# Splitting a weight load in three and moving the clearing transfers in an attention kernel

## The chip, the cores and the metric

The kernel runs on one core of one Trainium2 chip. The metric is the time of one launch in microseconds (us). The core has five instruction streams that run side by side and meet at semaphores: TensorE (PE, matrix products and transposes), VectorE (DVE), ScalarE (ACT), GpSimd (POOL) and SyncE (SP), which computes nothing here and issues most of the DMAs. "SPq" in a row is SP's stream; each stream is worked off strictly in its order.

## The reference

One decoder layer on x of 8 x 112 tokens x 512, in float32:

```python
x = _layernorm(x + attn(x, ...))     # latent attention: 16 heads, query rank 384, latent 128, rope part 64
x = _layernorm(x + xattn(x, ctx))    # cross-attention, 16 heads
x = _layernorm(x + ffn(x))           # 16 routed experts, the best 2 per token, and 2 shared experts

# inside attn
q_c, kv_c = rms_norm(x @ wq_down.T), rms_norm(x @ wkv_down.T)
q = concat(q_c @ wq_up.T, rope(q_c @ wq_rope.T)); k, v from kv_c @ wkv_up.T and rope(x @ wk_rope.T)
out = softmax(mask(q k^T * scale)) v @ wo.T
```

## The kernel before

Every float32 operand of a product is split into a high part (a rounding copy, nearly always on ACT) and a low part (source minus high part, nearly always on DVE), and a product is three matmuls: high x high, high x low, low x high. A weight thus goes HBM, buffer `stage`, high part, low part, product.

The first attention works on four groups of four heads (`NG = 4`, `GH = 4`). The weights of a group come in two loads into the one buffer `stage`: `wa`, 2816 columns of 128 partitions (1408 KB: the rope part of the query, the query's up-projection, the key's up-projection), and after it `wb`, 2560 columns (1280 KB: values and output). They are split in three pieces each:

```python
A_PIECES = [(0, A_UP), (A_UP, A_UP + 1024), (A_UP + 1024, A_SIZE)]   # 0:768, 768:1792, 1792:2816
B_PIECES = [(B_V, B_O), (B_O, B_O + 2 * D), (B_O + 2 * D, B_SIZE)]   # 0:512, 512:1536, 1536:2560
```

The order of the work of each engine is written out by hand, in lists of items (`ATT_PE`, `ATT_ACT`, `ATT_DVE`, `ATT_POOL`, lines 138 to 166). The list runs three times as the body of a loop, and a last list (`ATT_LAST_...`) ends the stage. In a body an item that is marked NEXT belongs to the next group: its weights are fetched and split while the present group's heads are still worked on. The items that matter here:

- `SA` 0 to 2: the split of the three pieces of `wa`; the high part on ACT counts `a_hi`, the low part on DVE counts `a_lo`. In ACT's body the next group's `SA` 0 and `SA` 1 stand next to each other, ahead of the transpose copy `T` 2.
- `SB` 0 to 2: the split of the three pieces of `wb`; the low part counts `bw_lo`. `SB` 0 of a group stands near the end of a body, `SB` 1 and `SB` 2 near the start of the next.
- `O` 0 and `E` 0 of the next group: the products that make the rope part of the queries, odd and even. They read piece 0 of `wa` (`a_lo` of one piece), and are PE's first work that needs the new weights. In PE's order `G` 3, `G` 4, `Z` 1, `S` 3, `S` 4, `T` 2 and `G` 5 come right ahead of `O` 0, then `B` 3, `Z` 2, `S` 5, `E` 0.
- `R` 0 and `R` 1: the split of one half (448 tokens) of the rotated queries into `ro_hi` (ACT) and `ro_lo` (POOL, which counts `rot_lo`). Each waits until the half before has been carried away (`pack_ld`).
- `G` j: scores of batch j. `G` 0 to 3 need the packed rope half 0 of their group, `G` 4 to 7 half 1.

SP's stream for this stage stands in lines 534 to 575. Ahead of the loop it issues the inputs, then `wa` of group 0 in one DMA (line 544), the residual input `acc` (line 545), `wb` of group 0, and `pack(0, 0)` and `pack(0, 1)`. `pack(g, half)` waits for `rot_lo` and issues 16 small DMAs (56 KB each, line 555) which carry a rotated half into `qr`. Then for g = 1, 2, 3:

1. wait until all three pieces of the old `wb` are split (line 569), then `wa` of group g in one DMA (line 570);
2. `load_b(g)`: wait until all three pieces of `wa` are split, then `wb` in one DMA (line 561);
3. `pack(g, 0)` and `pack(g, 1)`;
4. ten DMAs of 256 KB (`NZERO = 10`, line 575), HBM to HBM, that clear rows of `rows_in`, which the routed experts use much later (POOL waits for `zero_st` at line 781).

After the loop SP loads the weights of the cross-attention into `stage` (lines 589 to 591) and its context. `st_ld` is one semaphore for all `wa` and `wb` loads, counted up by 16 each.

Of the kernel before, what the change touches and what calls it, by code (L numbers as in the profile page):

```python
# [40 lines left out]
NZERO = -(-NBLK // (NG - 1))  # L41
# [275 lines left out]
def build(nc, d, rows_in, rows_out, out):  # L317
    with ExitStack() as ctx:
# [6 lines left out]
        def sem(name):  # L325
            return ctx.enter_context(nc.semaphore(name))
# [62 lines left out]
        def gap(name, upto):  # L389
# [70 lines left out]
        ix_i = sb("ix_i", [P, NBLK], I32)  # L460


        xo_ld, x2_ld, wk_ld, c_ld, acc_ld, st_ld, cx_ld, b_ld, zero_st, sc_st, out_st = map(
            sem, "xo_ld x2_ld wk_ld c_ld acc_ld st_ld cx_ld b_ld zero_st sc_st out_st".split())
        x_ld = [sem(f"x_ld{k}") for k in range(KD)]
        w_ld = [sem(f"w_ld{k}") for k in range(KD)]
        one_set, fw0_hi, fw0_lo = map(sem, "one_set fw0_hi fw0_lo".split())
        kb_ld = [sem(f"kb_ld{half}") for half in range(2)]
        pack_ld = [sem(f"pack_ld{half}") for half in range(2)]
        f_ld = [sem(f"f_ld{i}") for i in range(2)]  # L470
# [63 lines left out]
        @block.sync  # L534
        def _(sp):
            for k in range(KD):
                sp.dma_start(wd[:, k, 0:D], d["wdown"][:, k, 0:D]).then_inc(w_ld[k], 16)
                sp.dma_start(xT[:, k, 0:HALF], d["xT"][:, k, 0:HALF]).then_inc(x_ld[k], 16)
            sp.dma_start(xT[:, :, HALF:T], d["xT"][:, :, HALF:T]).then_inc(x2_ld, 16)
            sp.dma_start(wd[:, :, D:768], d["wdown"][:, :, D:768]).then_inc(wk_ld, 16)  # L540
            for dst, name in ((ident, "ident"), (maskf, "mask"), (wnorm, "wnorm")):
                sp.dma_start(dst[:, :], d[name]).then_inc(c_ld, 16)
            sp.dma_start(tab[:, :, :], d["tab"]).then_inc(c_ld, 16)
            sp.dma_start(stage[:, 0:A_SIZE], d["wa"][0, :, :]).then_inc(st_ld, 16)
            sp.dma_start(acc[:, :, :], d["xN"]).then_inc(acc_ld, 16)

            def pack(g, half):


                sp.wait_ge(rot_lo, 2 * g + half + 2)  # L550
                for part, src in enumerate((ro_hi, ro_lo)):
                    for o in range(2):
                        for h in range(GH):
                            row = 64 * part + 32 * o
                            sp.dma_start(  # L555
                                f32(qr[row:row + 32, h, half * HALF:(half + 1) * HALF]),
                                f32(src[32 * h:32 * h + 32, o, :])).then_inc(pack_ld[half], 16)

            def load_b(g):
                sp.wait_ge(a_lo, g * len(A_PIECES) + len(A_PIECES))  # L560
                sp.dma_start(stage[:, 0:B_SIZE], d["wb"][g, :, :]).then_inc(st_ld, 16)

            load_b(0)
            sp.wait_ge(kr_done, 4)
            pack(0, 0)
            pack(0, 1)
            with sp.Fori(1, NG) as g:

                sp.wait_ge(bw_lo, g * len(B_PIECES))
                sp.dma_start(stage[:, 0:A_SIZE], d["wa"][g, :, :]).then_inc(st_ld, 16)  # L570
                load_b(g)
                pack(g, 0)
                pack(g, 1)
                for i in range(NZERO):
                    sp.dma_start(rows_in[i, g - 1, :, :], d["zeros"]).then_inc(zero_st, 16)  # L575

            def load_x(g, lo, hi, loaded):
                sp.dma_start(stage[:, lo:hi], d["wx"][g, :, lo:hi]).then_inc(loaded, 16)

            def spread_keys(g, half):  # L580

                sp.wait_ge(x_free["K"], XJ.count(("K", half), g))
                for h in range(GH):
                    r = slice(DXH * h, DXH * (h + 1))
                    sp.dma_start(f32(kb[r, half, :, :, h, :]).rearrange("p a b s -> p (a b) s"),
                                 f32(kx[r, half, :, :]).rearrange("p a (b s) -> p (a b) s", b=HB))\
                      .then_inc(kb_ld[half], 16)

            sp.wait_ge(bw_lo, NG * len(B_PIECES))
            load_x(0, 0, X_O, xl_ld)  # L590
            load_x(0, X_O, X_SIZE, xo_ld)

            sp.wait_ge(a_free["B"], NG * GH)
            sp.dma_start(cx[:, :, :], d["ctxT"][:, :, 0:S]).then_inc(cx_ld, 16)
            sp.wait_ge(kz_set, 1)
            sp.wait_ge(a_free["G"], NG * B)
            for half in range(2):
                for a in range(2):
                    sp.dma_start(f32(kb[:, half, a, :, :, :]).rearrange("p b h s -> p b (h s)"),
                                 f32(kz[:, :]).unsqueeze(1).broadcast_to([P, HB, GH * S])).then_inc(kb_zero[half], 16)  # L600
            sp.wait_ge(kb_zero[0], 32)
            spread_keys(0, 0)

            sp.wait_ge(a_free["W"], 1 + NG * TT)
            for s in range(2):
                sp.dma_start(w1f[:, s, :], d["wf"][s, :, :]).then_inc(f_ld[s], 16)
            sp.wait_ge(kb_zero[1], 32)
            spread_keys(0, 1)
            with sp.Fori(1, NG) as g:
                sp.wait_ge(xl_lo, g)  # L610
                load_x(g, 0, X_O, xl_ld)
                spread_keys(g, 0)
                sp.wait_ge(xo_lo, g)
                load_x(g, X_O, X_SIZE, xo_ld)
                spread_keys(g, 1)

            sp.wait_ge(xl_lo, NG)
            sp.wait_ge(xo_lo, NG)
            for dst, name in ((gw[:, :, :], "gw"), (gb[:, :], "gb"),
                              (rev[:, :], "rev"), (e2[:, :], "e2"), (rt_c[:, :], "route")):  # L620
                sp.dma_start(dst, d[name]).then_inc(b_ld, 16)
            with sp.Fori(1, 2 * NF) as i:
                for s in range(2):

                    sp.wait_ge(fw_lo, 2 * i + s + 1)
                    sp.dma_start(stage[:, s * ROW:(s + 1) * ROW], d["wf"][2 * i + s, :, :])\
                      .then_inc(f_ld[s], 16)
            for t in range(TT):
                sp.wait_ge(ln_out, 2 * len(ROWS_ON_DVE) + t + 1)
                sp.dma_start(out[:, t, :], acc2[:, t, :]).then_inc(out_st, 16)  # L630
            sp.wait_ge(out_st, 16 * TT)
# [181 lines left out]
        def _(act):  # L813
# [36 lines left out]

            squares(0)
            act.wait_ge(in_lo, 2 * KD + 2)
            act.wait_ge(st_ld, 16)
            for lo, hi in A_PIECES:
                copy(wa_hi[:, lo:hi], stage[:, lo:hi]).then_inc(a_hi, 1)
            for b in range(HB):
                values(b)
# [38 lines left out]
            def att_step(item, g, at):  # L896
# [23 lines left out]
                    copy(ro_hi[:, :, :], rt[:, :, :]).then_inc(rot_hi, 1)  # L920
                elif kind == "SA":
                    lo, hi = A_PIECES[j]
                    act.wait_ge(st_ld, 32 * g + 16)
                    copy(wa_hi[:, lo:hi], stage[:, lo:hi]).then_inc(a_hi, 1)
                elif kind == "SB":
                    if j == 0:
                        act.wait_ge(st_ld, 32 * g + 32)

                        act.wait_ge(a_free["A"], AJ.count(("A", KQ - 1), g))
                    elif j == 1:  # L930

                        act.wait_ge(job_done, AJ.base(g))
                    copy(part_b(j, wa_hi, ws_hi), stage[:, slice(*B_PIECES[j])]).then_inc(bw_hi, 1)
                elif kind == "S":
                    probabilities(B * g + j, j)
                elif kind == "T":
                    transposed(B * g + j, j)
                elif kind == "Z":
                    act.wait_ge(z_done, B * g + j + 1)
                    copy(ZT_hi[:, :, j * S:(j + 1) * S],  # L940
                         ps[:, 4 + j % 2, 0:GH * S].rearrange("p (h s) -> p h s", h=GH))\
                        .then_inc(z_hi, 1)

                elif kind == "CX":
                    act.wait_ge(a_free["B"], NG * GH)
                    act.wait_ge(cx_ld, 16)
                    copy(cx_hi[:, :, :], cx[:, :, :]).then_inc(cxs_hi, 1)
                elif kind == "L":
                    split_l(0)
                elif kind == "ROOT1":  # L950
                    layernorm_root(0, j)
                elif kind == "ROW1":
                    row(0, j)
                elif kind == "SQRT":
                    function_ready(ACT.Sqrt)
                elif kind == "U1":
                    turned(0, j, x1T_hi)
                elif kind == "K":
                    x_step(item, 0, at)
# [1053 lines left out]
```

## Time and profile before

| | us |
|---|---|
| median of three runs | 851.8 |
| lowest and highest | 851.23, 852.64 |
| the profiled execution | 852.53 |
| its span | 850.7 |
| PE busy in the span | 820.5 |
| DVE, ACT, POOL busy | 531.7, 456.6, 241.2 |

The span is from the first to the last instruction of the profiled execution; its time has 1.83 us more. Busy PE is counted with modelled ends of pipelined matmuls: a matmul with 448 columns is listed with 0.36 us, but the next starts 0.20 us after it. Start-to-start times are therefore the ones to read on PE. "DMA to landing" is from the issue of a DMA until its semaphore says it is done. The granted clock is given as a share of 2.4 GHz.

### The profile page before, as it was taken

The page shows a single profiled execution, that of the slowest core. Times are in us where ns is not written, and L with a number is a line of the kernel's source. Part 1 is how long each engine was busy: PE and PEld are TensorE (multiplying, and loading weights), DVE is VectorE, ACT ScalarE, POOL GpSimd, SP SyncE. Part 2 cuts the span into 40 slices and gives each one's busy share as a digit, 9 for nine tenths or more (in the row PEclk, how much of TensorE's full clock was granted, in tenths as well). Part 3 has the DMA queues.
Part 4 walks back from the last instruction along what each step waited for, and adds up shares of the span by engine and source line. Part 5 has one row for each costly group of instructions (what it writes and reads, how often), then busy time and mean ns, then how long its engine had stood idle before and what let it go on. Part 6 is the DMA issues. An engine that isn't in the chain of part 4 may idle for free.

```text
span 850.7 us, 13303 instructions
## 1 busy us (share of the span) xinstructions
PE 820.5 (96%) x4270; PEld 700.7 (82%) x4270; DVE 531.7 (63%) x994; ACT 456.6 (54%) x1189; POOL 241.2 (28%) x284
## 2 busy tenths in 40 slices
PE   7999999799899999999997999999999999999997
PEld 5887888688688888888885888888888888889885
DVE  4757756654564677687787657265655655646466
ACT  6427535443554466977786616153755737547050
POOL 0142311032132132655654003502232322321420
PEclk9999999899989999999999999999999999999999
DMA  9113214230611346333112204534554655644422
GB/s 340 67 44 112 68 40 129 106 105 21 213 62 43 86 135 201 92 68 74 37 21 69 75 25 133 214 109 139 190 195 134 233 168 171 201 147 137 134 76 87
DMA packets 41598, 99.99 MB, mean 118 GB/s; under 512 B 15889, under 2 KB 23953, under 8 KB 39921
## 3 DMA queue, kind: packets, MB, share of 16 engines
q1 hardware_dynamic: 30496, 61.62, 22.9%
q0 software_dynamic: 11056, 37.79, 13.6%
q8 instruction: 27, 0.44, 0.2%
q14 instruction: 19, 0.15, 0.1%
HBM read 71.59 MB, written 20.97 MB: 109 GB/s over the span
## 4 chain that ended last, share of the span: by engine, by line
PE 78%; SPq 7%; DVE 4%; DMA 4%; ACT 3%; issue 3%; POOL 1%; DVEq 0%; ACTq 0%; POOLq 0%
PE ps L1549 63%; SPq L555 4%; DMA stage<-in_wa 3%; PE ps L1896 2%; PE ps L1570 2%; PE ps L1609 2%; PE ps L1712 2%; PE ps L1886 1%; SPq L575 1%; PE ps L1780 1%; ACT Pt L886 1%; POOL ro_lo L700 1%; DMA kb<-kx 1%; PE ps L1898 1%; PE ps L1720 1%
## 5 line engine op out<-in xcount | busy, mean ns | idle before, releaser
L641 POOL TENSOR_TENSOR Pt<-Pt,rowinv 112x448 f32<-112x448 f32 x64 | 59.6, 935 | 183.4 <-DVE rowinv L1153 183.2
L886 ACT ACTIVATE Pt<-ps,negmax 112x112 f32<-112x112 f32 x256 | 87.2, 358 | 26.9 <-DVE negmax L1146 26.4
L1549 PE MATMUL ps<-x2T_hi,ws_hi 128*128 128x448 f32 x256 | 95.2, 372 | 1.7 <-DVE x2T_lo L1090 1.7
L1549 PE MATMUL ps<-x2T_hi,ws_lo 128*128 128x448 f32 x256 | 93.6, 366 | 0.0
L1549 PE MATMUL ps<-x2T_lo,ws_hi 128*128 128x448 f32 x256 | 93.6, 366 | 0.0
L1549 PE MATMUL ps<-w_hi,h_hi 128*128 128x512 f32 x224 | 89.9, 401 | 0.0
L1549 PE MATMUL ps<-w_hi,h_lo 128*128 128x512 f32 x224 | 88.4, 395 | 0.0
L1549 PE MATMUL ps<-w_lo,h_hi 128*128 128x512 f32 x224 | 88.4, 395 | 0.0
L1017 ACT ACTIVATE hf<-ps,b 128x448 f32<-128x448 f32 x64 | 40.6, 634 | 88.0 <-PE ps L1549 68.7
L1090 DVE TENSOR_TENSOR h_lo<-hf,h_hi 128x448 fp32r<-128x448 f32 x64 | 39.9, 624 | 45.5 <-ACT h_hi L1018 45.0
L1435 DVE TENSOR_TENSOR acc<-ps,acc 128x512 f32<-128x512 f32 x56 | 38.5, 689 | 45.4 <-PE ps L1549 37.7
L1549 PE MATMUL ps<-qkT_hi,wa_hi 128*128 128x448 f32 x144 | 55.9, 388 | 11.0 <-DVE wa_lo L1090 9.5
L765 POOL DMA_INDIRECT wg<-in_wtab,ix_i x29 | 31.0, 1070 | 112.1 <-DVE ix_i L1420 61.3
L1163 DVE TENSOR_TENSOR acc<-ps,acc 128x512 f32<-128x512 f32 x56 | 38.6, 690 | 25.8 <-PE ps L1549 25.7
L815 ACT ACTIVATE PT_hi<-ps 112x448 fp32r<-112x448 f32 x64 | 34.7, 544 | 36.1 <-PE ps L1609 35.9
L1549 PE MATMUL ps<-qkT_hi,wa_lo 128*128 128x448 f32 x144 | 53.9, 374 | 0.0
L1549 PE MATMUL ps<-qkT_lo,wa_hi 128*128 128x448 f32 x144 | 53.8, 374 | 0.0
L886 ACT ACTIVATION_READ_ACCUMULATOR Pt<-ps,negmax 112x1 f32 x256 | 53.7, 210 | 0.0
L1549 PEld LDWEIGHTS ps<-x2T_hi,ws_hi 128*128 128x128 f32 x256 | 48.1, 188 | 6.5 <-POOL ws_lo L649 2.1
L1549 PEld LDWEIGHTS ps<-x2T_lo,ws_hi 128*128 128x128 f32 x256 | 48.2, 188 | 4.4
L1549 PEld LDWEIGHTS ps<-x2T_hi,ws_lo 128*128 128x128 f32 x256 | 48.1, 188 | 4.0
L1549 PEld LDWEIGHTS ps<-w_hi,h_lo 128*128 128x128 f32 x224 | 42.1, 188 | 10.2
(289 smaller groups left out, 2215.0 us busy)
## 6 DMA issues: line engine op xcount, KB each, us to landing
stage<-in_wf SPq DMA_DIRECT2D x30, 513.0 KB
rows_in<-in_zeros SPq DMA_DIRECT2D x30, 256.0 KB, 3.8
xs<-rows_in POOLq DMA_DIRECT2D x29, 256.0 KB, 4.2
rows_out<-yb POOLq DMA_DIRECT2D x29, 256.0 KB
stage<-in_wa SPq DMA_DIRECT2D x4, 1408.0 KB, 8.1
stage<-in_wb SPq DMA_DIRECT2D x4, 1280.0 KB, 5.5
qr<-ro_hi SPq DMA_DIRECT2D x64, 56.0 KB, 1.9
qr<-ro_lo SPq DMA_DIRECT2D x64, 56.0 KB, 1.9
```

The costliest lines, as they stand in the source:

```text
L555: sp.dma_start(f32(qr[row:row + 32, h, half * HALF:(half + 1) * HALF]), f32(src[32 * h:32 * h + 32, o, :])).then_inc(pack_ld[half], 16)
L641: nc.gpsimd.tensor_tensor(p, p, rowinv[0:S, b % 2, :].unsqueeze(2).broadcast_to([S, GH, S]), ALU.mult).then_inc(norm_done, 1)
L765: return pool.indirect_dma_start(dst, None, table, bass.IndirectOffsetOnAxis(ap=index, axis=0))
L815: return nc.scalar.activation(dst, src, ACT.Copy, **kw)
L886: last = nc.scalar.activation(Pt[0:S, b % 2, h * S:(h + 1) * S], ps[0:S, b % 2, h * S:(h + 1) * S], ACT.Exp, bias=negmax[0:S, b % 2, h:h + 1],
L1017: nc.scalar.activation(hf[:, q % 4, :], ps[:, q % 3, 0:HALF], ACT.Gelu, bias=bias)
L1090: return nc.vector.tensor_tensor(dst, src, f32(hi), ALU.subtract)
L1163: nc.vector.tensor_tensor(acc[:, t, :], ps[:, 6 + at.bank, :], acc[:, t, :], ALU.add)\
L1435: V.tensor_tensor(acc2[:, t, :], ps[:, 3 + m % 2, :], (acc2 if n else acc)[:, t, :], ALU.add)\
L1549: ins = mm(dst, w, x, start=start and i == 0, stop=stop and i == len(ops) - 1, skip_group_check=not (start and stop))
L1570: ins = mm(ps[0:S, b, :], w, x, start=k == 0 and i == 0, stop=k == KD - 1 and i == 2, skip_group_check=True)
L1609: ins = nc.tensor.transpose(ps[0:S, 2 + b % 2, h * S:(h + 1) * S], Pt[0:S, b % 2, h * S:(h + 1) * S], ident[0:S, 0:S])
```

## The change

The one DMA for `wa` of a group becomes three, one for each of `A_PIECES`, each with a semaphore of its own (`sa_ld[j]`). Inside the loop each of them waits only until those pieces of the old `wb` that lie under it are split: two for piece 0, all three for pieces 1 and 2. ACT waits per piece instead of for the whole. `wb` gets the semaphore `sb_ld`. The ten clearing DMAs move from the end of the loop's body to between `load_b(g)` and `pack(g, 0)`.

```diff
-            sp.dma_start(stage[:, 0:A_SIZE], d["wa"][0, :, :]).then_inc(st_ld, 16)
+            for (lo, hi), arrived in zip(A_PIECES, sa_ld):
+                sp.dma_start(stage[:, lo:hi], d["wa"][0, :, lo:hi]).then_inc(arrived, 16)
...
-                sp.dma_start(stage[:, 0:B_SIZE], d["wb"][g, :, :]).then_inc(st_ld, 16)
+                sp.dma_start(stage[:, 0:B_SIZE], d["wb"][g, :, :]).then_inc(sb_ld, 16)
...
-                sp.wait_ge(bw_lo, g * len(B_PIECES))
-                sp.dma_start(stage[:, 0:A_SIZE], d["wa"][g, :, :]).then_inc(st_ld, 16)
+                for j, (lo, hi) in enumerate(A_PIECES):
+                    under = sum(b < hi for b, _ in B_PIECES)
+                    sp.wait_ge(bw_lo, (g - 1) * len(B_PIECES) + under)
+                    sp.dma_start(stage[:, lo:hi], d["wa"][g, :, lo:hi]).then_inc(sa_ld[j], 16)
                 load_b(g)
+                for i in range(NZERO):
+                    sp.dma_start(rows_in[i, g - 1, :, :], d["zeros"]).then_inc(zero_st, 16)
                 pack(g, 0)
                 pack(g, 1)
-                for i in range(NZERO):
-                    sp.dma_start(rows_in[i, g - 1, :, :], d["zeros"]).then_inc(zero_st, 16)
...
-            act.wait_ge(st_ld, 16)
-            for lo, hi in A_PIECES:
+            for j, (lo, hi) in enumerate(A_PIECES):
+                act.wait_ge(sa_ld[j], 16)
                 copy(wa_hi[:, lo:hi], stage[:, lo:hi]).then_inc(a_hi, 1)
...
-                    act.wait_ge(st_ld, 32 * g + 16)
+                    act.wait_ge(sa_ld[j], 16 * g + 16)
...
-                        act.wait_ge(st_ld, 32 * g + 32)
+                        act.wait_ge(sb_ld, 16 * g + 16)
```

## Rows read from the trace of the kernel before

**Rows 1.** The page, part 1: busy time of each engine.

```profile
PE 820.5 (96%) x4270; PEld 700.7 (82%) x4270; DVE 531.7 (63%) x994; ACT 456.6 (54%) x1189; POOL 241.2 (28%) x284
```

**Rows 2.** Chain of waits, 45 to 330 us: start, duration, what.

```profile
128.09 0.95 ACT ro_hi L815
...
149.24 7.82 DMA stage<-in_wa
```

**Rows 3.** Timeline of SP: start, duration, engine, line, operation, count.

```profile
8.80 0.57 SPq L544 DMA_DIRECT2D stage<-in_wa  x1
...
77.18 0.36 SPq L570 DMA_DIRECT2D stage<-in_wa  x1
95.12 0.34 SPq L561 DMA_DIRECT2D stage<-in_wb  x1
104.16 4.95 SPq L555 DMA_DIRECT2D qr<-ro_hi  x8
...
131.43 4.94 SPq L555 DMA_DIRECT2D qr<-ro_hi  x8
...
141.64 6.94 SPq L575 DMA_DIRECT2D rows_in<-in_zeros  x10
...
206.79 4.94 SPq L555 DMA_DIRECT2D qr<-ro_hi  x8
...
282.24 4.95 SPq L555 DMA_DIRECT2D qr<-ro_hi  x8
```

**Rows 4.** Timeline of PE: first matmuls of `G` 4, `G` 5 and `O` 0.

```profile
83.98 0.44 PE L1712 MATMUL ps<-qa_hi,qkT_hi 128*112 128x448 f32 x1
...
85.25 0.47 PE L1549 MATMUL ps<-qkT_hi,wa_hi 128*128 128x448 f32 x1
...
150.22 0.37 PE L1712 MATMUL ps<-qa_hi,qkT_hi 128*112 128x448 f32 x1
...
153.19 0.44 PE L1712 MATMUL ps<-qa_hi,qkT_hi 128*112 128x448 f32 x1
...
158.97 0.74 PE L1549 MATMUL ps<-qkT_hi,wa_hi 128*128 128x448 f32 x1 [4.54 <-DVE wa_lo L1090]
...
228.52 0.44 PE L1712 MATMUL ps<-qa_hi,qkT_hi 128*112 128x448 f32 x1
...
234.75 0.74 PE L1549 MATMUL ps<-qkT_hi,wa_hi 128*128 128x448 f32 x1 [4.99 <-DVE wa_lo L1090]
```

**Rows 5.** Windows: PE, PEld, DVE, ACT, POOL busy; granted clock; DMA share; GB/s.

```profile
143.00:155.00 12.00, 11.41 (x65) 9.11 (x63) 8.92 (x16) 6.84 (x24) 1.87 (x2) 1.00 0.95 328
155.00:160.00 5.00, 1.03 (x3) 0.94 (x4) 2.02 (x3) 2.92 (x8) 0.00 (x0) 0.66 0.06 25
```

**Rows 6.** Timelines of DVE and of ACT: splits of `stage`.

```profile
139.70 1.22 DVE L1090 TENSOR_TENSOR ws_lo<-stage,ws_hi 128x1024 fp32r<-128x1024 f32 x1
143.44 1.22 DVE L1090 TENSOR_TENSOR ws_lo<-stage,ws_hi 128x1024 fp32r<-128x1024 f32 x1
...
19.68 2.73 ACT L815 ACTIVATE wa_hi<-stage 128x768 fp32r<-128x768 f32 x3
...
83.36 1.80 ACT L815 ACTIVATE wa_hi<-stage 128x768 fp32r<-128x768 f32 x2 [1.28 <-DMA stage<-in_wa]
...
157.09 1.79 ACT L815 ACTIVATE wa_hi<-stage 128x768 fp32r<-128x768 f32 x2 [5.79 <-DMA stage<-in_wa]
```

**Rows 7.** DMA issues by line: KB of each, median us to landing.

```profile
stage<-in_wx SPq DMA_DIRECT2D x4, 384.0 KB, 3.7
...
stage<-in_wa SPq DMA_DIRECT2D x1, 1408.0 KB, 9.5
...
rows_in<-in_zeros SPq DMA_DIRECT2D x10, 256.0 KB, 3.9
...
stage<-in_wb SPq DMA_DIRECT2D x1, 1280.0 KB, 5.6
```

More of the change, by code:

```diff
@@ L460, in build @@
         ix_i = sb("ix_i", [P, NBLK], I32)
-        xo_ld, x2_ld, wk_ld, c_ld, acc_ld, st_ld, cx_ld, b_ld, zero_st, sc_st, out_st = map(
-            sem, "xo_ld x2_ld wk_ld c_ld acc_ld st_ld cx_ld b_ld zero_st sc_st out_st".split())
+        xo_ld, x2_ld, wk_ld, c_ld, acc_ld, sb_ld, cx_ld, b_ld, zero_st, sc_st, out_st = map(
+            sem, "xo_ld x2_ld wk_ld c_ld acc_ld sb_ld cx_ld b_ld zero_st sc_st out_st".split())
         x_ld = [sem(f"x_ld{k}") for k in range(KD)]
@@ L467, in build @@
         one_set, fw0_hi, fw0_lo = map(sem, "one_set fw0_hi fw0_lo".split())
+        sa_ld = [sem(f"sa_ld{j}") for j in range(len(A_PIECES))]
         kb_ld = [sem(f"kb_ld{half}") for half in range(2)]
```

## The prediction

> **What bounds the kernel now.** I read the page first. PE is busy 820.5 of 850.7 us [rows 1], so only stretches in which PE stands still or runs slowly can give anything. Next the chain of waits, cut to the first attention: nearly all of it is PE, but in the second and the third body it leaves PE, goes along SP's small pack DMAs, then along the ten clearing DMAs, then into the load of `wa` [rows 2]. The timeline of SP says why: the clearing DMAs are issued from 141.64 to 148.58, and only then `wa`, at 149.24 [rows 2, 3]. It lands 7.82 us later, at 157.06. ACT has waited for it 5.79 us, and PE 4.54 us in this body and 4.99 us in the third [rows 4, 6]. In the first body nothing clears ahead of `wa` (issue at 77.18), ACT waits 1.28 us, and PE shows no idle time worth a mark [rows 3, 4, 6].
>
> PE pays once more after the wait: the granted clock of 155 to 160 us is 0.66, a mix of 1.2 and 2.4 GHz, where it was 1.00 before [rows 5]; PE had stood still for 4.54 us.
>
> The whole loss of a body can be read without separating the two. From the first matmul of `G` 5 to the first pack DMA of the next half, SP's start at 131.43, the three bodies do the same work: 131.43 - 83.98 = 47.45 us, 206.79 - 153.19 = 53.60, and 282.24 - 228.52 = 53.72 [rows 3, 4]. Against the first body the second loses 6.15 us and the third 6.27. The other part of the period is even: `G` 5 to `G` 5 is 69.21 us from the first body to the second and 75.33 from the second to the third, and these differ by 6.12, the same loss.
>
> **The change, part by part.** *Clearing DMAs out of the way of `wa`.* Once they are gone, SP is past its last pack DMA at about 141.5 (the next instruction begins at 141.64 [rows 3]). Piece 0 needs `SB` 0 and `SB` 1 of the old group split: the low part of `SB` 1 ends at 139.70 + 1.22 = 140.92 [rows 6], so piece 0 goes at about 141.7. Pieces 1 and 2 need `SB` 2, which ends at 143.44 + 1.22 = 144.66 [rows 6], so they go at 144.8 and, one issue of 0.36 [rows 3] and a wait later, at 145.3. Nothing else is queued on SP behind these waits but `load_b`, which in the first body came 95.12 - 77.18 = 18 us after the load of `wa` [rows 3].
>
> *When the pieces land.* Piece 0 has 384 KB; DMAs of that size took 3.7 us [rows 7], so it is there at 145.4. Pieces 1 and 2 are 1024 KB together, less than the 1280 KB of `wb`, which took 5.6 us [rows 7]: they are there by 150.4 at the latest for piece 1 and by 150.9 for piece 2. ACT comes to `SA` 0 at 157.09 - 5.79 = 151.30 and to `SA` 1 some 0.85 us later [rows 6]. So ACT waits for none. The slack is 5.9 us for piece 0 and 1.7 us for piece 1; piece 2 is split some 10 us later. Bounds of this step: nothing is left to wait for, or, if piece 1 landed as slowly as the whole `wa` does behind the clearing (7.82 us from 144.8), it is there at 152.6 and ACT loses 0.5 us per body, which also is late for nothing on PE but `E` 0. I take no wait.
>
> *What is late next.* Ahead of `O` 0 PE has `G` 5 (five matmuls, 0.20 us start to start and the first a little slower, about 1.1 us), and can start `O` 0 at about 154.3. ACT's high part of piece 0 would end at about 152.2; DVE's low part follows in its order behind other splits. In the first body the same order left 85.25 - 83.98 = 1.27 us between the two starts [rows 4], against 1.10 for the matmuls alone: 0.17 us lost with ACT 1.28 us late. The second and third bodies therefore come to the pace of the first, and slightly below it. Gain: 6.15 + 6.27 = 12.42 us, the slower clock included, since PE no longer stands still before these products.
>
> *The first body, and what the yardstick itself loses.* Here `wa` is issued at 77.18 behind the pack DMAs, not the clearing. Piece 0 lands at about 80.9 instead of 83.3, piece 1 at about 82 to 83; ACT comes to `SA` 0 at 82.08 [rows 3, 6, 7]. ACT's 1.28 us of waiting goes, all but some tenths. On PE that is worth at least the 0.17 us seen at `O` 0 and at most 1.28. The same amount is to be added in the other two bodies, for they were measured against this one. Three times 0.17 to 1.28 is 0.5 to 3.8 us; I take 0.4 each, nearer to the row at PE, 1.2 us in all.
>
> *Clearing DMAs in their new place.* `wb` is issued at 95.12, and SP then waited for `rot_lo` until 104.16 [rows 3]. Ten clearing DMAs take 6.94 us of issue [rows 3], from about 95.7 to 102.8. They fit with 1.3 us to spare, three times, as the distance between the two issues is set by PE's order. If that cover were gone, SP would be late with `pack(g, 0)`, which has 10.2 us of issue (131.43 to 141.64 is a whole pack [rows 3]), so ends near 114.5 to 115.5 and lands some 2 us later. The first who needs it is `R` 1 on ACT at 128.09 [rows 2], so about 11 us of cover stand behind the 1.3. Also the transfers: 1280 KB of `wb` and 2560 KB of clearing are 3.93 MB; at the 328 GB/s of a stretch full of such transfers [rows 5] that is 12.0 us, done at about 108. The pack DMAs issued from 104.16 stand behind them for up to 4 us, and the last ones, issued at 114 to 115, no longer. Cost 0.
>
> The rule that speaks against this change is in the Trainium skill, page "SBUF — State Buffer", section "The DMA setup-cost knee": each transfer pays some 2 us whatever its size, so one should coalesce. If the price were paid in series, an estimate from its fit (2 us + size / 436 GB/s) has pieces 1 and 2 at 144.8 + 2 x 3.2 = 151.2, still ahead of ACT's 152.15 for piece 1, and the sum stands. The trace disagrees with a series here: the clearing DMAs are issued every 0.70 us and land after 3.9 us each.
>
> *The start.* `wa` of group 0 becomes three DMAs: SP issues two more, at 0.57 us each [rows 3], so `acc` is asked for 1.1 us later; it is added to first in the loop, tens of us later. The whole `wa` landed at 8.80 + 9.5 = 18.3 [rows 3, 7], ACT took it from 19.68, and its third piece near 21.3 [rows 6]. Landing up to 1.1 us later is covered. Cost 0; without the cover it would be 1.1 us at most. A gain is excluded: ACT was busy with other work until 19.68.
>
> *The end of the stage.* In the last pass the clearing also stood in front of the cross-attention's weights (issue near 300.7). They come earlier now, but no engine was seen waiting for them. Worth 0. Semaphore renames cost nothing, and two more waits per group on ACT stand ahead of copies whose data is there.
>
> **Sum.** 12.42 + 1.2 = 13.6 us off the profiled execution: span 850.7 - 13.6 = 837.1, plus the 1.83 us around it 838.9. That execution lies 0.7 above the median of the runs shown (852.53 against 851.8), so the forecast for a median is 838.2. Nothing behind the stage depends on absolute time: it begins 13.6 us earlier and PE is the bound there as well.
>
> **Rivals.** *A, a part of the wait survives.* Piece 1 or DVE's low part comes late, or another wait inside ACT's order appears once PE no longer pauses (the pause let DVE and ACT catch up). For it: with ACT 1.28 us late `O` 0 was already late by 0.17 us, so the order has little over 1 us of slack there [rows 4, 6]. Against it: the first body shows the pace with ACT 1.3 us late. Half a us to 2 us per body at the place of the old wait, without the slow clock: 12.42 + 1.2 - 3 x 1.2 = 10.0 off, 841.8.
>
> *B, slower than before: the pack DMAs starve behind the clearing.* In the new place the clearing stands ahead of `pack(g, 0)` in the same queue. If HBM to HBM transfers were served one after another at their 3.9 us [rows 7], they would end at 100.7 + 39 = 140, the pack at about 142, and `R` 1 on ACT, due at 128.09 [rows 2], would be 14 us late; `pack(g, 1)` then is issued from about 145 and lands at 157, where `G` 4 wants it at 150.22 [rows 4]: PE loses about 7 us there beside what ACT's delay costs it before, say 12 in each of three groups, +36 - 13.6 = +22, 874. It decides from the point at which the backlog passes 11 us (the cover of `R` 1), and turns the sign when PE loses 4.5 us per group. Against it: the clearing DMAs are issued every 0.70 us and the `wa` behind all ten landed after 7.82 us, about 2 more than the 5.6 of a load of like size alone [rows 2, 7]: the backlog was 2 us, not 30. By the page's fit in series each would cost an estimated 2.6 us and the clearing 26, so the same would happen in a milder form.
>
> *C, the change does not remove the wait*, because `bw_lo` and not the clearing holds `wa`. Against it: `SB` 2 was split at 144.66, and `wa` issued at 149.24 [rows 3, 6]. If all pieces waited for it and landed only after the full 7.82 us, ACT would be served at 152.6, 1.3 us late, as in the first body: 12.4 us off, 839.4. So C lies inside the forecast's own bounds, and is no case of its own. That nothing is gained at all (within 0.2%) needs a second cost that eats 12 us, and I see none.
>
> **How the numbers follow.** Forecast 0.80, A 0.16, B 0.02, nothing gained 0.02. The forecast's own bounds are nothing and 3.8 beside the 12.42, so 839.4 to 835.6, and about 0.7 for the spread of medians. Range 836 to 841: it takes the forecast and the better half of A. A change of 0.2% (1.7 us) is what a measurement can tell from none. Faster 0.96, same 0.02, slower 0.02.
>
> **What would show it.** In the profile after: the three `wa` DMAs directly behind the pack DMAs, the second one about 3 us after the first in bodies two and three; the ten clearing DMAs behind `wb`; no wait of ACT for `stage<-in_wa` and none of PE for `wa_lo` above 0.3 us; `G` 5 to the next pack at 47 us in all three bodies; granted clock 1.00 there. It would be wrong if PE showed a new wait, above all for `pack_ld` at `G` 4 or for `wa_lo` at `E` 0, if ACT waited at `R` 1, or if the later stages took longer than the 850.7 - 282.2 = 568.5 us that they take from the third body's pack on.

## The result, and the profile after

The changed kernel took 838.58 us (median of four runs, 837.5 to 839.28), the kernel before 851.98 beside it (851.23 to 852.64): ratio 0.9837, 95% interval 0.9822 to 0.9851. In two further groups of runs the same kernel had 839.42 and 838.59 us, against 853.07 and 853.74 of the kernel before (ratios 0.984, interval 0.9822 to 0.9858, and 0.9818, interval 0.9804 to 0.9832). The forecast was 838.2 us, range 836 to 841.

The profiled execution took 837.5 us with a span of 835.7 us, 15.0 less than before. PE's busy time hardly changed, its share did (page, part 1, of the kernel after; compare [rows 1]):

```profile
PE 816.4 (98%) x4270; PEld 698.3 (84%) x4270; DVE 530.9 (64%) x994; ACT 456.7 (55%) x1189; POOL 241.1 (29%) x284
```

The timeline of SP of the kernel after, as in [rows 3]:

```profile
76.73 1.49 SPq L574 DMA_DIRECT2D stage<-in_wa  x3
93.78 0.33 SPq L563 DMA_DIRECT2D stage<-in_wb  x1
94.33 7.38 SPq L577 DMA_DIRECT2D rows_in<-in_zeros  x10
102.81 4.98 SPq L557 DMA_DIRECT2D qr<-ro_hi  x8
...
130.08 4.94 SPq L557 DMA_DIRECT2D qr<-ro_hi  x8
135.06 5.02 SPq L557 DMA_DIRECT2D qr<-ro_lo  x8
140.77 3.56 SPq L574 DMA_DIRECT2D stage<-in_wa  x3
...
198.65 4.94 SPq L557 DMA_DIRECT2D qr<-ro_hi  x8
...
267.17 4.95 SPq L557 DMA_DIRECT2D qr<-ro_hi  x8
```

Three things are to be seen. The load of `wa` stands right behind the pack DMAs, at 140.77 where it was at 149.24. The three pieces take 3.56 us to issue in body two, since the second waits for `SB` 2. And the issue of the clearing DMAs ends at 101.71, 1.1 us before the pack that follows them.

The timeline of PE of the kernel after: `G` 5 of the three bodies and `O` 0 of the first, as in [rows 4].

```profile
83.25 0.44 PE L1716 MATMUL ps<-qa_hi,qkT_hi 128*112 128x448 f32 x1
...
84.34 0.37 PE L1553 MATMUL ps<-qkT_hi,wa_hi 128*128 128x448 f32 x1
...
151.81 0.44 PE L1716 MATMUL ps<-qa_hi,qkT_hi 128*112 128x448 f32 x1
...
220.36 0.44 PE L1716 MATMUL ps<-qa_hi,qkT_hi 128*112 128x448 f32 x1
```

From `G` 5 to the first pack DMA of the next half it is now 130.08 - 83.25 = 46.83, 198.65 - 151.81 = 46.84 and 267.17 - 220.36 = 46.81 us, against 47.45, 53.60 and 53.72 before [rows 3, 4]. That is 0.62 + 6.76 + 6.91 = 14.3 us. Behind the third body's pack the span has 835.7 - 267.17 = 568.53 us more, before it was 568.46: in this profile the gain is kept to the end (other profiles lose 1.1 us of it there, see e3 below). The remaining 0.7 of the 15.0 us come from an earlier start (first `wb` load at 25.76 instead of 26.50), which is looked at below.

In body two ACT takes both pieces from `stage` without waiting (timeline of ACT of the kernel after, as in [rows 6]), and the clock holds (a window, columns as in [rows 5]). The other two bodies show no wait for `stage` either.

```profile
149.79 1.81 ACT L819 ACTIVATE wa_hi<-stage 128x768 fp32r<-128x768 f32 x2
```

```profile
155.00:160.00 5.00, 5.00 (x29) 4.20 (x28) 4.65 (x9) 2.26 (x4) 0.36 (x1) 1.00 0.00 0
```

### The profile page after: what moved, and what is told of

It reads as the page before. It is cut to its first block, busy times and chain, and to the rows that moved or that the text cites. A ratio compares the mean times of both kernels' runs of the same rounds, so it can differ in the third digit from the quotient of the medians.

```text
span 835.7 us, 13323 instructions
## 1 busy us (share of the span) xinstructions
PE 816.4 (98%) x4270; PEld 698.3 (84%) x4270; DVE 530.9 (64%) x994; ACT 456.7 (55%) x1189; POOL 241.1 (29%) x284
## 4 chain that ended last, share of the span: by engine, by line
PE 89%; DVE 4%; ACT 3%; issue 1%; DMA 1%; SPq 1%; DVEq 0%; ACTq 0%
PE ps L1553 71%; PE ps L1716 4%; PE ps L1900 2%; PE ps L1574 2%; PE ps L1613 2%; PE ps L1890 2%; PE ps L1724 1%; PE ps L1784 1%; ACT Pt L890 1%; DMA kb<-kx 1%; PE ps L1902 1%; SPq L589 1%; DVE stats L1173 1%; PE ps L1568 1%; PE ps L1605 0%
## 5 line engine op out<-in xcount | busy, mean ns | idle before, releaser
L1553 PE MATMUL ps<-qkT_hi,wa_hi 128*128 128x448 f32 x144 | 54.2, 377 | 1.3 <-DVE wa_lo L1097 0.6
```

Of the source, the lines that this page charges most:

```text
L1553: ins = mm(dst, w, x, start=start and i == 0, stop=stop and i == len(ops) - 1, skip_group_check=not (start and stop))
```

## Experiments

All are timed against the kernel before on the same chip, and each trace shown is one execution. Theory A is the prediction's: what cost the time was how late `wa` arrived against ACT, because of the clearing ahead of it on SP.

### One half of the change at a time

**after_again** is the changed kernel once more.

> The changed kernel once more, on the same chip as the three that follow, as their yardstick. Both theories: 838.6 us again, within 1 us. Beyond that: its first `wb` load was issued at 25.76 us where the kernel before had 26.50. If that 0.74 us belongs to the change, it is there again; if it is scatter between executions, the issue may come anywhere between 25.7 and 26.6.

839.42 us (839.31 to 840.06), ratio 0.984 (0.9822 to 0.9858).

**e1_clear_only**: the kernel before, with only this edit.

```diff
                 load_b(g)
+                for i in range(NZERO):
+                    sp.dma_start(rows_in[i, g - 1, :, :], d["zeros"]).then_inc(zero_st, 16)
                 pack(g, 0)
                 pack(g, 1)
-                for i in range(NZERO):
-                    sp.dma_start(rows_in[i, g - 1, :, :], d["zeros"]).then_inc(zero_st, 16)
```

> Only the clearing DMAs are moved, `wa` stays one DMA behind all of the old `wb`. Theory A (the clearing ahead of `wa` in SP's queue was the whole cause): `wa` goes about 4.6 us earlier against PE's order, when `SB` 2 is split, and lands 6.2 us later, within 0.5 us of when ACT comes for it. Bodies two and three run at the pace of the first, and the first keeps ACT's 1.3 us wait: some 0.65 us per body worse than the full change at most, so 838.8 to 840.6 us. Theory B (the early first piece carries the gain): PE still waits 3 us or more for `wa_lo` in bodies two and three, 845 us or more.

839.12 us (837.75 to 839.59), ratio 0.9832 (0.9813 to 0.9851): all of the gain that can be measured. SP's and ACT's timelines of this kernel:

```profile
65.38 4.95 SPq L555 DMA_DIRECT2D qr<-ro_hi  x8
...
130.68 4.95 SPq L555 DMA_DIRECT2D qr<-ro_hi  x8
144.09 0.34 SPq L570 DMA_DIRECT2D stage<-in_wa  x1
...
199.25 4.94 SPq L555 DMA_DIRECT2D qr<-ro_hi  x8
```

```profile
150.39 1.81 ACT L815 ACTIVATE wa_hi<-stage 128x768 fp32r<-128x768 f32 x2
```

The one load goes as soon as `SB` 2 is split, at 144.09, and it lands 6.0 us later; ACT begins at 150.39 with no idle time marked before it, so the cover is only 0.3 us.

These two traces also say what the clearing did to `wa`. Counted from the first pack DMA of the half before, `wa` is issued at 13.41 us here and at 17.81 us in the kernel before, 4.4 us later, because SP issues the clearing first; and it lands after 7.82 us there against 6.0 here, 1.8 us more, while the clearing's own bytes are moved. No run issued the clearing from another engine's stream, so these two parts are read from the traces and not separated by an experiment.

From pack to pack body two takes 199.25 - 130.68 = 68.57 us, exactly as in the full change (198.65 - 130.08 = 68.57). In the first body ACT still waits 1.3 us, and its pack to pack time is 65.30 us; the kernel before had 65.27, the full change 64.67. So the split into three is worth 0.6 us in the trace, once, which is less than the runs can tell. In bodies two and three e1 has all of the gain without the split (its third body takes 68.59 us, the full change 68.52).

**e2_split_only**: the changed kernel with the clearing DMAs back at the end of the body.

> Only the split into three DMAs, the clearing DMAs stay at the end of the loop's body. Theory A: all three pieces are issued behind the clearing, the first lands some 5 us later instead of 7.8, so ACT waits about 2.7 us and PE about 1.6 us in bodies two and three; the clock may still fall. Of the 14 us some 8 to 10 come back: 842 to 844.5 us. Theory B: the first piece is early enough whatever stands ahead of it, 839 us or less.

847.22 us (845.72 to 849.22), ratio 0.9931 (0.9911 to 0.995). This missed the expected 842 to 844.5, on theory A's side of the line but with less gain. ACT's, then PE's timeline of body two:

```profile
154.92 0.84 ACT L819 ACTIVATE wa_hi<-stage 128x768 fp32r<-128x768 f32 x1 [3.72 <-DMA stage<-in_wa]
```

```profile
156.81 0.47 PE L1553 MATMUL ps<-qkT_hi,wa_hi 128*128 128x448 f32 x1 [2.46 <-DVE wa_lo L1094]
```

The first piece was issued at 149.17 and ACT could begin 5.7 us later, where I had reckoned with 5; with nothing ahead of it such a piece lands 3.1 us after its issue (below). PE stands 2.46 us in body two and 2.20 in body three instead of the 1.6 reckoned, and the clock falls as well (0.76 in the five us from 155, 0.90 in the next five). From pack to pack the two bodies take 4.3 and 4.0 us more than in the changed kernel.

The Trainium skill, page "Perfetto Trace Analysis", section "DMA Optimizations", says that splitting a DMA can let the work complete sooner if the DMA engines are generally idle. The runs here do not bear out that condition: with the DMA engines 0.95 busy from 150 to 155 us the split won back 5.9 of 14 us, and with the clearing gone 0.6. With the clearing gone there was little left to win: ACT's 1.28 us of waiting in the first body.

**e3_first_whole**, and once more as **e3_again**: the changed kernel, with only the first load, ahead of the loop, in one DMA again (ACT's waits follow it, not shown).

```diff
-            for (lo, hi), arrived in zip(A_PIECES, sa_ld):
-                sp.dma_start(stage[:, lo:hi], d["wa"][0, :, lo:hi]).then_inc(arrived, 16)
+            sp.dma_start(stage[:, 0:A_SIZE], d["wa"][0, :, :]).then_inc(sa_ld[0], 16)
```

> The changed kernel, but `wa` of group 0 in one DMA as before; the loop is untouched. If the 0.74 us by which the start came earlier belongs to the split of the first load, this kernel is 0.7 us slower than the changed one and issues its first `wb` at about 26.5 us. If it was scatter, the two are the same within 0.3 us. Both theories on the clearing: no difference in the bodies, 68.5 us each.

837.83 us (837.27 to 838.97), ratio 0.9824 (0.9805 to 0.9843). Its first `wb` load was issued at 25.84 us, and in e1, which also has the whole first load, at 25.73; the changed kernel had 25.76 in one profile and 26.27 in the next. The earlier start does not belong to the split. The time, however, lay 1.6 us below that of the changed kernel beside it, which neither expectation had, so both were run again:

> The changed kernel as the yardstick of this group: 838 to 839.5 us. Its profile before had 1.2 us more between the last load ahead of the routed layer and the first output DMA (384.6 us against 383.3 in all others). If that belongs to single executions, it may be there or not; the kernel with the first load whole (next) is then equal to this one within 0.5 us.

> The changed kernel with `wa` of group 0 in one DMA, once more: in its first group of runs it had 837.83 us against 839.42 of the changed kernel. If the split of the first load costs something (descriptors while the DMA engines are full), it is again 1 us or more faster than the yardstick. If that was scatter of where a program's runs fall, the two lie within 0.5 us.

838.59 us (837.33 to 839.34) for the changed kernel, 838.74 (837.48 to 839.11) for the other: no difference, ratios 0.9818 (0.9804 to 0.9832) and 0.9822 (0.9809 to 0.9836). What remains is a scatter of about 1.1 us behind the third body: from its pack to the end it is 568.3 to 568.6 us in six profiles (the kernel before, the changed kernel's first, e1, e2 and both of e3) and 569.5 to 570.1 in the other six (the changed kernel's other two and e4 to e7).

The clock goes with it. In the two us from 176 us behind the pack, at the end of the cross-attention, the granted clock is 0.50 to 0.62 in the second six and 1.00 in the first six. Three of the first six have a slow stretch 4 us earlier, three have none. The window at 176 us in the changed kernel's first profile, then in its third (columns as in [rows 5]):

```profile
443.17:445.17 2.00, 1.80 (x9) 0.97 (x7) 1.97 (x5) 1.41 (x3) 1.84 (x4) 1.00 0.00 0
```

```profile
443.96:445.96 2.00, 2.00 (x9) 1.81 (x8) 1.37 (x3) 1.46 (x3) 1.84 (x4) 0.50 0.00 0
```

So the same kernel has its slow stretch at one place or 4 us later, and only the profiles with the later one have the longer end. That is read from twelve profiles side by side; no experiment moved the stretch, and what places it stays open.

### How much lateness costs what

**e4_half**: the kernel before, with five of the ten clearing DMAs moved behind `load_b` and five left.

> `wa` in one DMA, five of the ten clearing DMAs moved behind `load_b`, five left at the end of the body. Theory A (what counts is how late `wa` arrives against ACT): five DMAs are 3.5 us of issue, so `wa` goes at about 145 in body two and lands some 7 us later, at 152 to 152.5; ACT came for it at 149.8, so it waits 2.2 to 2.7 us, PE some 1.5 us, and the clock stays up or falls for part of a us. Loss against the changed kernel 1.5 to 2.5 us in each of two bodies and 0.6 in the first: 842 to 844 us. If a clearing DMA cost in proportion (theory C: 7.2 us per body for ten), it would be 845.5 us.

844.84 us (843.11 to 846.13), ratio 0.9889 (0.9873 to 0.9906), a little above theory A's range and by time alone as near to the proportional theory C. Within the kernel the two bodies differ. SP's timeline, then PE's in body two and body three:

```profile
131.61 4.96 SPq L555 DMA_DIRECT2D qr<-ro_hi  x8
141.83 3.39 SPq L577 DMA_DIRECT2D rows_in<-in_zeros  x5
145.89 0.34 SPq L570 DMA_DIRECT2D stage<-in_wa  x1
...
202.17 4.94 SPq L555 DMA_DIRECT2D qr<-ro_hi  x8
...
274.41 4.95 SPq L555 DMA_DIRECT2D qr<-ro_hi  x8
```

```profile
156.01 0.47 PE L1551 MATMUL ps<-qkT_hi,wa_hi 128*128 128x448 f32 x1 [1.39 <-DVE wa_lo L1092]
```

```profile
227.05 0.47 PE L1551 MATMUL ps<-qkT_hi,wa_hi 128*128 128x448 f32 x1 [1.87 <-DVE wa_lo L1092]
```

The windows of the two bodies, columns as in [rows 5]:

```profile
155.00:160.00 5.00, 3.90 (x20) 3.31 (x21) 4.05 (x8) 4.26 (x13) 0.93 (x1) 1.00 0.00 0
225.00:230.00 5.00, 3.13 (x11) 2.64 (x11) 2.83 (x5) 4.00 (x12) 0.93 (x1) 0.79 0.00 0
```

Against 68.5 us of the changed kernel, body two takes 202.17 - 131.61 = 70.56, 2.0 more, and body three 72.24, 3.7 more. `wa` landed 8.2 us after its issue in body two (7 had been reckoned) and 8.8 us in body three; ACT waited 2.64 and 3.12 us, and PE stood for 1.39 and 1.87. That is 0.5 us of the difference of 1.7. The larger part is the clock: 1.00 all through 155 to 165 us, but 0.79 and 0.87 in the two stretches of five us from 225. From the fourth matmul of `O` 0 on, the same ten matmuls up to the start of the tenth take 1.91 us in body two (156.73 to 158.64) and 3.43 in body three (227.76 to 231.19), 1.5 us more, of which 0.3 is won back at `E` 0, where body two waits and body three does not. Half the clearing in front thus costs 2.0 us in a body when the clock holds and 3.7 when it does not; all of it costs 6.8 and 6.9. The profiled execution was the slowest of the four, 846.13 us with a mean granted clock of 0.993; the fastest had 843.11 with 0.997. So theory A's range holds where the clock holds; what the expectation had too small is the cost of the clock.

**e5_wait_all**: the changed kernel, every piece waits for the whole of the old `wb`.

```diff
-                    under = sum(b < hi for b, _ in B_PIECES)
+                    under = len(B_PIECES)
```

> The changed kernel, but all three pieces of `wa` wait until the whole of the old `wb` is split, so that the first piece goes 3 us later, at 143.4 in body two, and lands near 146.5; ACT comes for it at 149.8. Theory A: no difference, 838.6 us within 0.7. If the early first piece matters, PE or ACT shows a wait and the time rises by 1 us or more.

838.57 us (837.66 to 839.43), ratio 0.9834 (0.9817 to 0.985): no difference. `wa` went at 144.15 instead of 140.77 and nobody waited for it. The finer wait of the first piece is worth nothing here.

### The cover behind the clearing

**e6_clear_x2** and **e7_clear_x4** have twenty and forty clearing DMAs per body in the new place; `rows_in` is made larger, and the new ones clear spare rows.

```diff
-                for i in range(NZERO):
+                for i in range(4 * NZERO):
```

> The changed kernel with twenty clearing DMAs in place of ten in each body, the ten new ones into spare rows that nothing reads. SP is busy with them for 14 us, so `pack(g, 0)` goes about 5.5 us later than in the changed kernel and lands at about 120 in body one; `R` 1 on ACT comes for it at 127. Theory A (11 us of cover behind the pack): no difference, 838.6 us within 0.7. Theory D (the clearing costs by its traffic or by starving the pack DMAs, the rival of the prediction): 3 us or more slower.

838.47 us (837.58 to 840.29), ratio 0.9827 (0.981 to 0.9844): twice the clearing is free. The pack moved from 102.81 to 108.80 in body one, and ACT's `R` 1 began at 126.69, without a wait. That is 30 DMAs of 256 KB more in the kernel, with PE none the slower.

> The changed kernel with forty clearing DMAs in each body, thirty of them into spare rows. SP needs 28 us for them, from 94.4 to 122.5 in body one, then `pack(1, 0)` until about 132.7, landing near 135; `R` 1 on ACT comes for it at 127. Theory A: ACT stands 8 us at `R` 1, `pack(g, 1)` goes 8 us late and PE waits at `G` 4; 5 to 10 us in each of three bodies, so 854 to 868 us. If the time does not move, the cover is larger than read, and the wait of `R` 1 for the pack is not what limits.

866.73 us (865.98 to 867.19), ratio 1.0167 (1.015 to 1.0184): slower than the kernel before. SP's, ACT's and PE's timeline in body one:

```profile
94.93 28.93 SPq L577 DMA_DIRECT2D rows_in<-in_zeros  x40
123.99 5.13 SPq L557 DMA_DIRECT2D qr<-ro_hi  x8
129.17 5.25 SPq L557 DMA_DIRECT2D qr<-ro_lo  x8
139.81 4.94 SPq L557 DMA_DIRECT2D qr<-ro_hi  x8
```

```profile
136.52 0.95 ACT L819 ACTIVATE ro_hi<-rt 128x896 fp32r<-128x896 f32 x1 [9.07 <-DMA qr<-ro_lo]
```

```profile
139.12 0.71 PE L1716 MATMUL ps<-qa_hi,qkT_hi 128*112 128x448 f32 x1 [7.01 <-DVE qa_lo L1094]
```

The pack ends its issue at 134.42 and has landed 2 us later; ACT, in order, stands 9.07 us at `R` 1, and behind it wait the copies that PE's next scores need. PE stands 7.01 us and then works at a lower clock for a while (0.78 from 140 to 145 us). The bodies take 73.81, 76.81 and 78.11 us from pack to pack, 9.1, 8.2 and 9.6 more than in the changed kernel: 27.0 us, and the medians differ by 28. This is the path of the prediction's slower rival. The transfers do queue up here (the first eight pack DMAs land after 6.9 us, median, against 2.4 in the changed kernel), but the last ones do not, so what makes the pack late is the time SP needs to issue forty DMAs, not a serial transfer.

## Why the prediction was right

- *The number*: nearer than its parts, by luck. The forecast was 13.6 us off span and median alike. The profiled span fell by 15.0 us: 14.3 in the bodies, where the sum had 13.6, and 0.7 from an earlier start that does not belong to the change. The median fell by 13.4, because the profiled execution was the fastest of its four, 1.1 us below their median, where the forecast had taken over from the kernel before that it lies 0.7 above.
- *What bounds*: right. With the clearing out of the way of `wa` (e1) the second and third body run at the pace of the first or slightly faster, as was said.
- *The 12.42 us against the first body*: right, measured by the same two marks.
- *What the yardstick itself loses*: the step that was mis-sized. It was taken at 0.4 us in each of three bodies within bounds of 0.17 and 1.28, and measured 0.62. With it the sum in the bodies is 14.3 us, not 13.6. The prediction read PE's loss at `O` 0 alone. Set side by side, the two traces show 0.27 us lost there (0.18 in the start of `O` 0, 0.1 in its first matmul) and 0.34 at `E` 0. From the transposes ahead of it to the first matmul of `E` 0 it was 0.64 us (88.50 to 89.14), and it is 0.32 now (87.50 to 87.82). `E` 0 did not wait for piece 1, as the prediction had it, but for DVE, which had the result of `O` 0 still to multiply (`ru`) before PE had the bank for its own result free; DVE and PE of the kernel before:

```profile
87.94 1.15 DVE L1224 TENSOR_TENSOR ru<-ps,tab 128x448 f32<-128x448 f32 x2
```

```profile
89.14 0.47 PE L1549 MATMUL ps<-qkT_hi,wa_hi 128*128 128x448 f32 x1
```

DVE ended `ru` at 89.09, in the kernel after at 87.56, before PE was through with the transposes. The prediction put nothing for this into the term. Nor did it say which part of the change brings this gain in bodies two and three; e1 has it there without the split.

- *When the pieces land*: on the safe side. In the window from 135 to 155 us the first piece landed 3.1 us after its issue (3.7 assumed), the other two 4.0 (5.6 was the bound). The Trainium skill (page "SBUF — State Buffer", section "The DMA setup-cost knee") has a fit that gives an estimated 2.9 us for the first size and 3.2 us for the second. The trace is 0.2 and 0.8 us above it, and a series of fixed costs was seen nowhere.
- *The clearing in its new place*: right. SP had 1.1 us of spare time (1.3 expected), and the first pack DMAs behind the clearing landed after 2.4 us, median, instead of 1.9. The larger cover behind it was read as 11 us: 6 us of delay cost nothing (e6). In e7 the pack came 20.6 us later, counted from the load of `wb` (29.61 us against 9.03), and left ACT standing 9.07, which puts the cover at 11.5.
- *The clock*: the slow stretch went with the wait. The prediction lumped wait and clock together, which was sound, as both went. The expectations of e2 and e4, which had to price a shorter wait, left the cost of the lower clock out or too small, e2's the length of the stand as well, and both times came out above their range.
- *The parts of the change*: the prediction gave the clearing's move nearly everything without saying that the rest is worth nothing. The runs say so: e1 alone reaches 839.12 us, and neither the split of the first load (e3) nor the first piece's earlier wait (e5) can be measured. No run beat the changed kernel beyond its scatter; e1 is the simpler kernel with the same time.
- *Rival A*, a surviving wait, did not occur. *Rival B* did not occur with the clearing as it is or twice as long, and did with four times as much; nothing between was run. *Rival C*: `bw_lo` does hold `wa` in e1 and e5, at 144.1, and it costs nothing, as ACT comes at about 150.

## What to carry to other kernels

When a stream that only issues DMAs appears in the chain of waits, look at what it issues just before the late load: work that nobody needs soon (here 7 us of clearing) belongs where that stream waits anyway. The same bytes cost nothing there; in front of the load they held it back by 4.4 us with their issue and 1.8 with their transfer. Measure such a loss between two marks of PE's own order in a body with the wait and one without, and remember that the body taken as the yardstick may be late too, at more than one product. Before splitting a load, see whether it is late because of its size or because of what is queued ahead of it: here the order gave 14 us and the split 0.6.

## What was not expected of the hardware

In the first attention a stand of PE of 1.39 us left the granted clock at 1.00 (e4, body two), and stands of 1.87 (e4, body three), 2.46 (e2) and 4.54 us (the kernel before) were followed by 0.79, 0.76 and 0.66 in the stretch of five us around them. The smallest of these with a drop cost nearly as much by the clock (1.5 us) as by the stand. The drop can come when PE is at work again: in e4 the clock is 1.00 from 226 to 227 us, where PE stands, 0.93 in the next us and 0.50 from 228 to 231, where it is busy.

The length of a stand alone does not say what the clock does. At the end of the cross-attention e3_first_whole and e3_again, the same kernel, have the same stands of PE (0.28 or 0.26, then 0.54 or 0.55, then 0.83 or 0.85 us), and in three stretches of 2 us from 170 us behind the third body's pack, the clock is 0.73, 0.50 and 0.91 in the one and 1.00 throughout in the other. Both spans are 835.8 us. Each of the four stands above was read from one body of one profile, so 1.39 and 1.87 us bound no threshold.
